# Five stores issued from SyncE's queue instead of ScalarE's

## The chip, the cores and the metric

The kernel runs on the 8 cores of one Trainium2 chip. Each core does the same program on its own data; there is no traffic between cores. The metric is the device time of the slowest core in microseconds.

## The reference

An input x of 4 x 8192 x 1024 (float32) goes through four blocks, each with a layernorm in front and a residual sum behind:

```python
# LN is a layernorm over the last axis
proj = LN(x) @ W_proj.T;  delta, Bs, Cs, residual = split(proj, 4)
delta = softplus(delta @ W_delta.T + b_delta)
y = exp(delta * A) * B * sum_t(xn * Cs) + cumsum_t(delta * B) * sum_t(Cs)
x = x + y + residual * D                       # scan block
x = x + LN(x) @ (W + up @ lora @ down).T + b   # feed forward
q, k, v = LN(x) @ Wq.T + bq, ... Wk ..., ... Wv ...
x = x + softmax(q @ k.T / 32) @ v              # attention over 8192 positions
x = x + LN(x) @ (W + up @ lora @ down).T + b   # feed forward again
```

## The kernel before

Two cores share one of the four sequences. Each core computes keys and values for all 8192 positions (64 tiles of 128 rows, `NT`), and queries and output for its own 4096 (32 tiles, `NQ`). Between the stages, intermediate tiles go to scratch tensors in device memory (names that begin with `sc_`) and are loaded again.

The program is written as lists, one for each engine. `Sched.add` puts an instruction and the semaphore waits ahead of it at the end of an engine's list, and each engine works through its own list in order. `dma(q, out, in, waits, ch)` (L171; every issue is recorded as L177) puts a transfer into the list of "sync" (the SP queue) or of "scalar" (the ACT queue, which ScalarE's own sequencer issues between its computations); `ch` is the semaphore that counts its landing. So the order in which the Python code calls `add` and `dma` is the order of every queue, and a transfer that has to wait stands in front of everything that was added later to the same engine.

Stages, in order of time:

1. *Weights*, loaded through SP and cast by POOL (GpSimd), to about 330 us.
2. *First stage*, 64 tiles (`p1B`, to about 1290 us): three projections on TensorE; softplus of delta on ScalarE (L440, L442); column sums. Each tile stores `sc_delta` (L446) and `sc_res` (L472), both through ACT. The loads of x (`xb`) go through SP, five tiles ahead, and the layernorm of tile i+3 stands behind the store of `sc_res` of tile i on ScalarE's list.
3. *Scan stage*, 64 tiles (`p2A` to `p2C`, to about 3500 us). All of its transfers are on SP.
4. *Query projection* (to about 3735 us), 8 groups of 4 tiles. `prep_group` loads normalized tiles (`xq_in`, SP), transposes them on TensorE (L186) and copies them on ScalarE (L817). Then come 8 x 8 matmuls (L834) with their evictions on ScalarE (L841), and four stores of `sc_qT` (L847, through ACT). Their pieces in memory are 256 bytes long.
5. *Attention*, 4 rounds (`r` = 0 to `KR`-1 = 3), each over a quarter of the keys. A round begins with keys and values of its 16 tiles (L884, L903; loads of `xq_in` again), and then takes the 32 query tiles as steps. A step has three parts. `qS(step)` issues the load of `qT_t` (SP), from round 1 on the load of `zl` (the running sum of the round before, SP), in round 3 also of `x2l` (SP), and then the scores on TensorE (L944), their maxima on VectorE (L954) and the exponentials on ScalarE (L981). `qB(step)` transposes the probabilities (L1013) and copies them on ScalarE (L1021, L1024). `qC(step)` multiplies by the values (L1037) into `PC`, and VectorE writes `zs` (L1046 in round 0, L1051 after it). In rounds 0 to 2, `qC` ends with the store of `sc_z` (L1060, ACT). In round 3 it goes on with a layernorm, the feed forward matmuls (L1086), VectorE's sum (L1093), POOL's sum `s_out` (L1098) and the store of `out` (L1102, ACT).

The order of the parts differs between rounds:

```python
# rounds 0 to 2                         # round 3
qS(step + 2)                            qC(step)
qB(step + 1)                            qS(step + 2)
qC(step)                                qB(step + 1)
```

So in rounds 0 to 2 TensorE does the scores of step s+3 right after the values of step s; in round 3 it does the scores of step s+2 right after L1086 of step s. The buffer `qT_t` is double: its load for a step waits for the scores two steps earlier. `zl` has three buffers and waits for `zs` three steps earlier.

Of the kernel before, what the change touches and what calls it, by code (L numbers as in the profile page):

```python
# [76 lines left out]
def build(phases=3, dbg=False, cut=None):  # L77
# [31 lines left out]
    sc_delta = dS("sc_delta", [NT, 128, 1024])  # L109
    sc_res = dS("sc_res", [NT, 128, 1024])  # L110
# [4 lines left out]
    sc_qT = dS("sc_qT", [NQ, 128, 8, 128], BF16)  # L115
    sc_z = dS("sc_z", [NQ, 128, 1024])
# [140 lines left out]
    try:  # L257
# [119 lines left out]
        if phases >= 1:  # L377
# [35 lines left out]
            def p1B(i):  # L413
# [29 lines left out]
                    delta_f[pp][:, :], e1_f[pp][:, :], AF.Ln, bias=1.0), (SM(mex),),  # L443
                    inc=("s", 1))
                mk[("sp", i)] = mln
                mk[("dst", i)] = dma("scalar", sc_delta[i, :, :], delta_f[p][:, :], ch=f"sdl{p}")  # L446
                mcb = sch.add("scalar", lambda e, pp=p: e.copy(cs_bf[pp][:, :], PB[:, :]),
                              (TM(mcs), GM(mk.get(("m", i - 1), 0)),
                               TM(mk.get(("colsum", i - 1), 0))), inc=("s", 1))
# [10 lines left out]
                for n in range(2):  # L460
                    for k in range(8):
# [7 lines left out]
                    res_f[pp][:, :], PA[:, :]),  # L469
                    (TM(mrs), mk.get(("rst", i - 2))), inc=("v", 1))  # L470
                mk[("resev", i)] = mrev
                mk[("rst", i)] = dma("scalar", sc_res[i, :, :], res_f[p][:, :], (VM(mrev),),  # L472
                                     ch=f"sre{p}")
                mcl = None
                for n in range(2):
# [309 lines left out]
        if phases >= 3:  # L785
# [41 lines left out]
            for g in range(8):  # L827
                pg = g % 2
                mev = prep_group(range(4 * g, 4 * g + 4), pg)
                for c in range(8):  # L830
                    half = c % 2
                    mq = None
                    for k in range(8):
                        mq = sch.add("tensor", lambda e, cc=c, kk=k, hh=half, pp=pg: e.matmul(  # L834
                            PA[:, hh * 512:(hh + 1) * 512],
                            WqT[:, kk * 1024 + cc * 128: kk * 1024 + (cc + 1) * 128],
                            xg3T[pp][:, kk, :], start=(kk == 0), stop=(kk == 7)),
                            ((SM(mev), GM(mwq)) if c == 0 else
                             (SM(mk3.get(("qev", g, c - 2), 0)),)) if k == 0 else (),
                            inc=("t", 1) if k == 7 else None)  # L840
                    mqe = sch.add("scalar", lambda e, cc=c, hh=half, pp=pg: e.activation(  # L841
                        qsp[pp][:, cc, :], PA[:, hh * 512:(hh + 1) * 512],
                        AF.Identity, bias=s_bqT[:, cc:cc + 1], scale=1.0),
                        (TM(mq), mk3.get(("qst", g - 2))), inc=("s", 1))
                    mk3[("qev", g, c)] = mqe
                for t in range(4):
                    mk3[("qst", g)] = dma("scalar", sc_qT[4 * g + t, :, :, :],  # L847
                                          qsp[pg][:, :, t * 128:(t + 1) * 128],
                                          (SM(mk3[("qev", g, 7)]),) if t == 0 else (),
                                          ch=f"sq{pg}")  # L850
# [23 lines left out]
            for r in range(KR):  # L874
# [154 lines left out]
                def qC(step):  # L1029
                    qi = step - r * NQ  # L1030
                    p = step % 2
                    ac = 3 + 3 * (step % 2)
                    mpe = mk3[("pev", step)]
                    mpv = None
                    for j in range(16):
                        for n in range(2):
                            mpv = sch.add("tensor", lambda e, jj=j, nn=n, pp=p: e.matmul(  # L1037
                                PC[:, nn * 512:(nn + 1) * 512], pt_sb[pp][:, jj, :],
                                v_res[:, jj * 1024 + nn * 512: jj * 1024 + nn * 512 + 512],
                                start=(jj == 0), stop=(jj == 15)),  # L1040
                                ((SM(mpe), VM(mk3.get(("zco", step - 1), 0)),
                                  VM(mk3.get(("mo1", step - 1), 0)))
                                 if (j == 0 and n == 0) else ()),
                                inc=("t", 1) if (j == 15 and n == 1) else None)
                    if r == 0:
                        mz = sch.add("vector", lambda e, pp=p: e.tensor_copy(zs[pp][:, :],  # L1046
                                                                             PC[:, :]),
                                     (TM(mpv), mk3.get(("zst", step - 2))), inc=("v", 1))
                    else:
                        mz = sch.add("vector", lambda e, pp=p, z3=step % 3, a_=ac:  # L1050
                                     e.scalar_tensor_tensor(  # L1051
                            zs[pp][:, :], zl[z3][:, :], pstat[:, a_:a_ + 1], PC[:, :],
                            ALU.mult, ALU.add),
                            (TM(mpv), mk3.get(("lz", step)), SM(mk3[("al", step)]),
                             mk3.get(("zst", step - 2)),
                             GM(mk3.get(("moo", step - 2), 0))),
                            inc=("v", 1))
                    mk3[("zco", step)] = mz
                    if r < KR - 1:
                        mk3[("zst", step)] = dma("scalar", sc_z[qi, :, :], zs[p][:, :],  # L1060
                                                 (VM(mz),), ch=f"sz{p}")
                    else:
                        mli = sch.add("vector", lambda e, q_=qi: e.reciprocal(
                            pstat[:, 5:6], l_run[:, q_:q_ + 1]),
                            (mk3[("lr", step)],), inc=("v", 1))
                        mx3 = sch.add("vector", lambda e, pp=p: e.scalar_tensor_tensor(
                            x3b[pp][:, :], zs[pp][:, :], pstat[:, 5:6], x2l[pp][:, :],
                            ALU.mult, ALU.add),
                            (VM(mli), mk3.get(("lx2", step)),
                             GM(mk3.get(("moo", step - 2), 0))), inc=("v", 1))  # L1070
                        mk3[("x3", step)] = mx3
                        if dbg:
                            mk3[("zdbg", step)] = dma("scalar", sc_z[qi, :, :], zs[p][:, :],
                                                      (VM(mx3),), ch=f"sz{p}")
                        mxn4 = ln(x3b[p], xn4b[p], st4[p],
                                  (VM(mx3), TM(mk3.get(("tp4", step - 1), 0))))
                        mtp4 = transposes8(PT1, xn4b[p], (SM(mxn4),))
                        mk3[("tp4", step)] = mtp4
                        mev4 = sch.add("scalar", lambda e, pp=p: e.copy(xn4T[pp],
                                                                        PT1[:, :, :]),  # L1080
                                       (TM(mtp4),), inc=("s", 1))
                        mk3[("ev4", step)] = mev4
                        mf2 = None
                        for n in range(2):
                            for k in range(8):
                                mf2 = sch.add("tensor", lambda e, nn=n, kk=k, pp=p: e.matmul(  # L1086
                                    PC[:, nn * 512:(nn + 1) * 512], xn4T[pp].tensor[:, kk, :],
                                    W_eff[:, kk * 1024 + nn * 512: kk * 1024 + nn * 512 + 512],
                                    start=(kk == 0), stop=(kk == 7)),
                                    (SM(mev4), VM(mk3[("zco", step)])) if (n == 0 and k == 0)  # L1090
                                    else (),
                                    inc=("t", 1) if (n == 1 and k == 7) else None)
                        mo1 = sch.add("vector", lambda e, pp=p: e.tensor_add(  # L1093
                            zs[pp][:, :], PC[:, :], s_bfbc[:, :]),
                            (TM(mf2), GM(mk3.get(("moo", step - 2), 0)),
                             mk3.get(("zdbg", step))), inc=("v", 1))
                        mk3[("mo1", step)] = mo1
                        moo = sch.add("gpsimd", lambda e, pp=p: e.tensor_add(  # L1098
                            s_out[pp][:, :], zs[pp][:, :], x3b[pp][:, :]),
                            (VM(mo1), mk3.get(("ost", step - 1))), inc=("g", 1))  # L1100
                        mk3[("moo", step)] = moo
                        mk3[("ost", step)] = dma("scalar", out_d[qi * 128:(qi + 1) * 128, :],  # L1102
                                                 s_out[p][:, :], (GM(moo),), ch=f"so{p}")

                qS(r * NQ)
# [138 lines left out]
```

How the kernel before makes its waits and increments, by code:

```python
        def f(eng):  # L1144
            for item in sch.prog[name]:
                if item[0] == "w":
                    eng.wait_ge(sems[item[1]], item[2])
                else:
                    _, fn, inc = item
                    ins = fn(eng)
                    if inc is not None:
                        ins.then_inc(sems[inc[0]], inc[1])
```

## Time and profile before

| | us |
|---|---|
| median of 2 runs | 7386.89 |
| the two runs | 7283.85, 7489.93 |
| the profiled execution | 7288.19 |
| its span (slowest core, core 1) | 7286.6 |
| spans of the 8 cores | 7252.1 to 7286.6 |
| mean granted TensorE clock, each core | 0.784 |

The span is the time from the first to the last instruction of the slowest core; the profiled execution's time has 1.6 us around it. Busy shares over the whole span are TensorE 60%, ScalarE 34%, VectorE 22%, POOL 18%. They are averages over stages with different limits, so the stages have to be read apart. The granted clock is the share of full speed (2.4 GHz) that TensorE was given; 0.5 is 1.2 GHz. In the rows, SPq and ACTq are the issues of transfers by SP and by ScalarE. Us to landing is the time from the issue to the arrival of the data.

### The profile page before, as it was taken

What the parts mean: (1) busy time and instruction counts of PE and PEld (TensorE: products, weight loads), DVE (VectorE), ACT (ScalarE), POOL (GpSimd) and SP (SyncE); (2) the same over time, 40 slices, a digit from 0 to 9 for tenths busy, and PEclk for the clock granted to TensorE, in tenths of its full rate; (3) what the DMA queues carried; (4) which work ended last, traced back from release to release, by engine and by line L of the source; (5) the groups of instructions that cost most, each with busy time, mean ns of one, the idle gap of its engine ahead of it and who ended that gap; (6) DMA issues with size and microseconds to landing.
All of it is one profiled execution on the core that took longest, in us unless ns stands there. A gap on an engine that the chain in (4) does not pass through costs nothing.

```text
span 7286.6 us, 65385 instructions; the slowest of 8 cores (7252.1 to 7286.6 us)
## 1 busy us (share of the span) xinstructions
PE 4391.3 (60%) x20288; PEld 1954.9 (27%) x20288; DVE 1639.0 (22%) x2744; ACT 2501.2 (34%) x4418; POOL 1323.1 (18%) x611
## 2 busy tenths in 40 slices
PE   3788887122222222222578997999899865555555
PEld 1333333000000000000234443444344322222222
DVE  0322222122222222222002221332233122222221
ACT  0555553133333333333323342333233223222222
POOL 2222222443344344443100000000000000000000
PEclk8899998555555555555789999999999977777777
DMA  4222221311211111111221111222122101111110
GB/s 131 93 98 96 96 99 68 117 65 65 75 69 65 65 61 51 61 51 52 69 52 36 55 53 38 79 87 73 45 87 88 59 35 41 41 41 41 41 48 25
DMA packets 183211, 475.82 MB, mean 65 GB/s; under 512 B 51149, under 2 KB 51278, under 8 KB 182868
## 3 DMA queue, kind: packets, MB, share of 16 engines
q1 hardware_dynamic: 112564, 328.75, 14.2%
q10 hardware_dynamic: 70304, 142.89, 5.0%
q8 instruction: 168, 2.75, 0.2%
q14 instruction: 175, 1.43, 0.1%
HBM read 295.12 MB, written 176.42 MB: 65 GB/s over the span
## 4 chain that ended last, share of the span: by engine, by line
PE 46%; ACT 17%; POOL 11%; DVE 10%; DMA 8%; issue 5%; SPq 2%; ACTq 1%; DVEq 0%; POOLq 0%
PE PC L1037 13%; PE PA L944 6%; PE PB L944 6%; DMA p2B<-sc_delta 5%; PE PA L884 3%; PE PB L903 3%; PE PA L420 3%; PE PC L1086 3%; PE PT L186 2%; POOL p2g L650 2%; POOL p2D L644 2%; POOL p2D L673 2%; POOL g_bf L451 2%; ACT L208 2%; DVE st L191 2%
## 5 line engine op out<-in xcount | busy, mean ns | idle before, releaser
L1037 PE MATMUL PC<-v_res,pt_sb 128*128 128x512 bf16 x4096 | 994.8, 405 | 285.3 <-ACT pt_sb L1024 280.1
L1098 POOL TENSOR_TENSOR s_out<-zs,x3b 128x1024 f32<-128x1024 f32 x32 | 75.0, 2343 | 3695.9 <-DVE zs L1093 3695.9
L1037 PEld LDWEIGHTS PC<-v_res,pt_sb 128*128 128x128 bf16 x4096 | 415.3, 103 | 813.9 <-issue 412.3
L186 PE MATMUL PT<-s_id,xn2b 128*128 128x128 bf16 x512 | 64.8, 307 | 755.4 <-ACT xn2b L212 755.4
L944 PE MATMUL PA<-kT_res,qT_t 128*128 128x512 bf16 x2048 | 470.7, 384 | 28.5 <-ACT P_bf L981 22.6
L944 PE MATMUL PB<-kT_res,qT_t 128*128 128x512 bf16 x2048 | 462.9, 379 | 0.0
L712 PE MATMUL PB<-W_eff,xn2T 128*128 128x512 bf16 x1024 | 361.5, 531 | 85.5 <-ACT xn2T L700 84.0
L644 POOL TENSOR_TENSOR p2D<-p2B,s_A1bc 128x1024 f32<-128x1024 f32 x64 | 149.6, 2338 | 1014.4 <-DMA p2B<-sc_delta 1013.8
L655 PE MATMUL PA<-p2g,s_tri 128*128 128x512 bf16 x64 | 32.4, 609 | 455.1 <-POOL p2g L650 455.1
L648 ACT ACT_TABLE_LOAD x61 | 78.3, 1283 | 643.8 <-POOL p2D L644 643.8
L451 POOL TENSOR_TENSOR g_bf<-delta_f,s_B1bc 128x1024 bf16<-128x1024 f32 x64 | 150.0, 2344 | 794.4 <-ACT delta_f L442 794.4
L944 PEld LDWEIGHTS PA<-kT_res,qT_t 128*128 128x128 bf16 x2048 | 201.5, 99 | 277.6 <-issue 43.0
L903 PE MATMUL PB<-WvT,xg3T 128*128 128x512 bf16 x1024 | 231.3, 379 | 71.3 <-DVE v_res L913 71.3
L420 PE MATMUL PA<-W_dd,xnT 128*128 128x512 bf16 x1024 | 268.8, 422 | 3.5 <-DVE xnT L409 3.5
L884 PE MATMUL PA<-xg3T,WkT 128*128 128x512 bf16 x1024 | 253.0, 413 | 23.5 <-ACT xg3T L817 23.5
L186 PEld LDWEIGHTS PT<-s_id,xn2b 128*128 128x128 bf16 x512 | 49.6, 138 | 810.5 <-issue 810.5
L944 PEld LDWEIGHTS PB<-kT_res,qT_t 128*128 128x128 bf16 x2048 | 200.4, 98 | 241.7
L655 PE MATMUL PC<-p2g,s_tri 128*128 128x512 bf16 x64 | 32.4, 609 | 385.4 <-POOL p2g L650 385.4
L913 DVE TENSOR_TENSOR v_res<-PB,s_bvbc 128x1024 bf16<-128x1024 f32 x64 | 78.4, 1225 | 811.9 <-PE PB L903 811.9
L954 DVE TENSOR_REDUCE cmax<-PB 128x1 f32<-128x512 f32 x256 | 177.1, 692 | 263.7 <-PE PB L944 263.7
L1051 DVE SCALAR_TENSOR_TENSOR zs<-zl,pstat,PC 128x1024 f32<-128x1024 f32 x96 | 122.9, 1280 | 487.9 <-PE PC L1037 487.9
L434 PE MATMUL PB<-WcT,xnT 128*128 128x512 bf16 x1024 | 231.5, 379 | 0.0
(164 smaller groups left out, 6929.9 us busy)
## 6 DMA issues: line engine op xcount, KB each, us to landing
sc_z<-zs ACTq DMA_DIRECT2D x96, 512.0 KB, 4.7
zl<-sc_z SPq DMA_DIRECT2D x96, 512.0 KB, 5.0
xb<-x SPq DMA_DIRECT2D x64, 512.0 KB, 3.5
sc_delta<-delta_f ACTq DMA_DIRECT2D x64, 512.0 KB, 2.6
sc_res<-res_f ACTq DMA_DIRECT2D x64, 512.0 KB, 2.6
p2A<-x SPq DMA_DIRECT2D x64, 512.0 KB, 4.9
p2B<-sc_delta SPq DMA_DIRECT2D x64, 512.0 KB, 5.6
p2C<-sc_res SPq DMA_DIRECT2D x64, 512.0 KB, 6.5
```

Source lines behind the costliest of these rows:

```text
L186: e.transpose(o, i_, s_id[:, :]),
L420: mdp = sch.add("tensor", lambda e, nn=n, kk=k, qq=q3: e.matmul(PA[:, nn * 512:(nn + 1) * 512], xnT[qq][:, kk, :], W_dd[:, kk * 1024 + nn ...
L434: mcs = sch.add("tensor", lambda e, nn=n, kk=k, qq=q3: e.matmul(PB[:, nn * 512:(nn + 1) * 512], xnT[qq][:, kk, :], WcT[:, kk * 1024 + nn * ...
L451: mg0 = sch.add("gpsimd", lambda e, pp=p: e.tensor_mul(g0_bf[pp][:, :], delta_f[pp][:, :], s_B1bc[:, :]), (SM(mln), TM(mk.get(("colsum", i ...
L644: mei = sch.add("gpsimd", lambda e, pp=p: e.tensor_mul(D_[pp][:, :], B_[pp][:, :], s_A1bc[:, :]), (VD(mk2[("ldl", i)]), GM(mr2) if i == 0 ...
L712: mf1 = sch.add("tensor", lambda e, nn=n, kk=k, pp=p: e.matmul(PB[:, nn * 512:(nn + 1) * 512], xn2T[pp][:, kk, :], W_eff[:, kk * 1024 + nn ...
L884: mq = sch.add("tensor", lambda e, cc=c, kk=k, hh=half, pp=pg: e.matmul(PA[:, hh * 512:(hh + 1) * 512], WkT[:, kk * 1024 + cc * 128: kk * ...
L903: mv = sch.add("tensor", lambda e, nn=n, kk=k, tt=t, pp=pg: e.matmul(PB[:, nn * 512:(nn + 1) * 512], xg3T[pp][:, kk, tt * 128:(tt + 1) * 128],
L944: e.matmul(o[:, of:of + 512], qT_t[pp][:, cc, :], kT_res[:, cc, nn * 512:(nn + 1) * 512], start=(cc == 0), stop=(cc == 7)),
L954: mrx = sch.add("vector", lambda e, nn=n, o=ps_, of=off: e.reduce_max(cmax[:, nn:nn + 1], o[:, of:of + 512], AX), (TM(msmm),), inc=("v", 1))
L1037: mpv = sch.add("tensor", lambda e, jj=j, nn=n, pp=p: e.matmul(PC[:, nn * 512:(nn + 1) * 512], pt_sb[pp][:, jj, :], v_res[:, jj * 1024 + n ...
L1086: mf2 = sch.add("tensor", lambda e, nn=n, kk=k, pp=p: e.matmul(PC[:, nn * 512:(nn + 1) * 512], xn4T[pp].tensor[:, kk, :], W_eff[:, kk * 10 ...
```

## The change

Five stores go into SP's list instead of ScalarE's, at the same places of the program: `sc_delta` and `sc_res` of each tile of the first stage, the four `sc_qT` of each group of the query projection, `sc_z` of each step of rounds 0 to 2, and `out` of each step of round 3. The store of `sc_delta`, which had stood behind its producer on ScalarE itself, gets an explicit wait for it; the other stores keep the waits they had. The two small stores `sc_hi` and `sc_lo` stay on ACT.

```diff
-                mk[("dst", i)] = dma("scalar", sc_delta[i, :, :], delta_f[p][:, :], ch=f"sdl{p}")
+                mk[("dst", i)] = dma("sync", sc_delta[i, :, :], delta_f[p][:, :],
+                                     (SM(mln),), ch=f"sdl{p}")
...
-                mk[("rst", i)] = dma("scalar", sc_res[i, :, :], res_f[p][:, :], (VM(mrev),),
+                mk[("rst", i)] = dma("sync", sc_res[i, :, :], res_f[p][:, :], (VM(mrev),),
                                      ch=f"sre{p}")
...
                 for t in range(4):
-                    mk3[("qst", g)] = dma("scalar", sc_qT[4 * g + t, :, :, :],
+                    mk3[("qst", g)] = dma("sync", sc_qT[4 * g + t, :, :, :],
                                           qsp[pg][:, :, t * 128:(t + 1) * 128],
                                           (SM(mk3[("qev", g, 7)]),) if t == 0 else (),
                                           ch=f"sq{pg}")
...
                     if r < KR - 1:
-                        mk3[("zst", step)] = dma("scalar", sc_z[qi, :, :], zs[p][:, :],
+                        mk3[("zst", step)] = dma("sync", sc_z[qi, :, :], zs[p][:, :],
                                                  (VM(mz),), ch=f"sz{p}")
...
-                        mk3[("ost", step)] = dma("scalar", out_d[qi * 128:(qi + 1) * 128, :],
+                        mk3[("ost", step)] = dma("sync", out_d[qi * 128:(qi + 1) * 128, :],
                                                  s_out[p][:, :], (GM(moo),), ch=f"so{p}")
```

## Rows read from the trace of the kernel before

**Rows 1.** The page, granted TensorE clock in 40 slices of the span, in tenths

```profile
PEclk8899998555555555555789999999999977777777
```

**Rows 2.** Stretches (rounds 0, 1, 3): length, PE, PEld, DVE, ACT, POOL, clock, DMA

```profile
3900.00:4370.00 470.00, 461.12 (x2495) 223.34 (x2494) 136.51 (x223) 181.16 (x413) 0.00 (x0) 1.00 0.15 51
...
4580.00:5050.00 470.00, 461.70 (x2515) 224.75 (x2516) 152.90 (x335) 183.38 (x406) 0.00 (x0) 0.99 0.26 88
...
6600.00:7286.00 686.00, 374.07 (x1578) 161.97 (x1576) 142.46 (x268) 190.33 (x357) 37.48 (x16) 0.73 0.11 38
```

**Rows 3.** Timeline of a step of round 1: start, duration (us), engine, line, operation

```profile
4729.47 3.62 PE L944 MATMUL PA<-kT_res,qT_t 128*128 128x512 bf16 x16
4729.88 1.28 DVE L1051 SCALAR_TENSOR_TENSOR zs<-zl,pstat,PC 128x1024 f32<-128x1024 f32 x1 [1.31 <-PE PC L1037]
...
4731.29 0.32 SPq L177 DMA_DIRECT2D zl<-sc_z  x1
...
4731.71 0.38 SPq L177 DMA_DIRECT2D qT_t<-sc_qT  x1
...
4744.18 3.62 PE L944 MATMUL PA<-kT_res,qT_t 128*128 128x512 bf16 x16
```

**Rows 4.** Chain of waits in the same step: start, duration, engine, tile, line

```profile
4722.73 6.91 PE PC L1037 x32
4729.63 3.45 PE PA L944 x16
```

**Rows 5.** Timeline, a step of round 0

```profile
4004.67 1.23 DVE L1046 COPY zs<-PC 128x1024 f32<-128x1024 f32 x1 [2.58 <-PE PC L1037]
```

**Rows 6.** Tile qT_t, issue to landing: round 0, round 1, round 3

```profile
DMA to landing us min/median/max: 2.5/2.6/3.1
...
DMA to landing us min/median/max: 4.6/5.0/6.1
...
DMA to landing us min/median/max: 3.6/4.1/4.9
```

**Rows 7.** Timeline, a step of round 3

```profile
6508.02 9.95 PE L1037 MATMUL PC<-v_res,pt_sb 128*128 128x512 bf16 x32 [8.85 <-ACT pt_sb L1024]
...
6529.93 5.78 PE L1086 MATMUL PC<-W_eff,pt_sb 128*128 128x512 bf16 x16 [1.36 <-ACT pt_sb L1079]
...
6535.55 3.62 PE L944 MATMUL PA<-kT_res,qT_t 128*128 128x512 bf16 x16
...
6537.25 2.35 POOL L1098 TENSOR_TENSOR s_out<-zs,x3b 128x1024 f32<-128x1024 f32 x1 [42.00 <-DVE zs L1093]
...
6539.68 0.34 ACTq L177 DMA_DIRECT2D out<-s_out  x1
```

**Rows 8.** Stretches of the query projection, columns as in rows 2

```profile
3601.40:3606.80 5.40, 0.05 (x2) 0.04 (x2) 0.00 (x0) 1.02 (x2) 0.00 (x0) 0.90 1.00 243
3606.80:3610.20 3.40, 2.02 (x16) 1.51 (x16) 0.00 (x0) 3.03 (x3) 0.00 (x0) 0.50 0.60 154
```

**Rows 9.** Timeline between two groups of the query projection

```profile
3601.41 4.13 ACTq L177 DMA_DIRECT2D sc_qT<-qsp  x4
3605.64 4.47 ACT L817 COPY xg3T<-PT 128x1024 bf16<-128x1024 bf16 x4 [4.30 <-issue]
3606.80 2.16 PE L186 MATMUL PT<-s_id,xq_in 128*128 128x128 bf16 x16 [5.35 <-ACT xg3T L817]
```

**Rows 10.** Chain of waits from round 0 into the projection of round 1

```profile
4389.38 0.91 PE PT L186 x16
...
4390.35 3.69 DMA xq_in<-sc_xn
```

**Rows 11.** Timeline, a tile of the first stage

```profile
805.76 16.91 SPq L177 DMA_DIRECT2D xb<-x  x2
...
814.61 0.33 ACTq L177 DMA_DIRECT2D sc_res<-res_f  x1
816.16 1.06 ACT L193 ACTIVATE s_sqscr<-xb 128x1024 bf16<-128x1024 f32 x1 [3.45 <-POOL m_bf L455]
```

## Prediction, on record before the change was run

> **What bounds the kernel now.** I read the views in this order: the clock line of the page, the busy times by stage, one step of the attention in order of time, the chain of waits of the same step, and then the issue-to-landing times of the query load.
>
> The clock line [rows 1] shows a kernel of several stages: high in the first fifth, low in the middle (the scan stage, which this change does not touch), full in three blocks of the attention, and about 0.73 in the last one. The stage table [rows 2] says what limits each. In rounds 0, 1 and 2 of the attention TensorE is busy for 461 of 470 us at the full clock: it is the bound, and whatever makes it wait is added to the end. In round 3 it is busy for 374 of 686 us, at 0.73: there TensorE, VectorE and ScalarE hand one tile to each other in a chain, so a delay of a link is added too.
>
> One step of round 1 [rows 3] is where the change decides. The queue of SP issues `zl` when VectorE has written `zs`, and 0.42 us later `qT_t`. That `qT_t` is not for the matmuls that run at this moment. They began at 4729.47, before it was issued; it is for the scores one step (14.71 us) later. The chain [rows 4] shows it: the last value matmul at 4722.73 takes 6.91 us and the scores follow at 4729.63 with no wait between. All of the load's landing time is hidden by a step of work.
>
> **The change, part by part.** Nothing is computed differently. Five stores leave ScalarE's queue for SP's, and SP works through its list in order: an issue that waits holds up every later one.
>
> *Rounds 0 to 2, `sc_z`.* Order on TensorE: scores(s+3) right behind values(s). Order on SP from now on: the store of step s, which waits for `zs`(s), and behind it the loads of `qT_t`(s+3) and `zl`(s+3). In the kernel before, `qT_t`(s+3) stood behind a wait for step s-1 at most. Now it stands behind one for step s, whose result comes after the very matmul that the scores follow. So scores(s+3) wait: from the end of the values at 4729.63 to the start of `zs` 0.25 us, `zs` itself 1.28, its signal to the issue 0.13, the store's place in the queue 0.42 (the spacing of two issues), then the landing L, then 0.13 to start TensorE (an estimate, the same as from `zs` to the issue): 2.2 us + L [rows 3, 4]. In round 0 the eviction is 1.23 us [rows 5], which gives 2.16 + L.
>
> L is read from the landing times of this same load [rows 6]: 2.6 us alone (round 0), 4.1 behind one other 512 KB transfer on its queue (round 3), 5.0 with a 512 KB load ahead of it and a 512 KB store beside it (rounds 1 and 2). The new queue has one 512 KB store ahead and, from round 1 on, `zl` behind: that is round 3's pattern, so 4.1. In round 0 nothing follows it, and I take the middle of 2.6 and 4.1, 3.4. The bounds are 2.6 and 5.0.
>
> [...]
>
> Stalls: 2.16 + 3.4 = 5.6 us in round 0, 2.2 + 4.1 = 6.3 in rounds 1 and 2. In each round the first store stands behind the load for its third step, so 29 loads (steps 3 to 31) are late: 29 x 5.6 = 162, 58 x 6.3 = 365.
>
> *The clock.* A wait of this length costs more than itself. In the query projection TensorE sat idle for 5.35 us [rows 9]; the granted clock of that stretch was 0.90, so it fell from full to half towards its end, and was 0.50 after it [rows 8]. 0.50 is 1.2 GHz, 1.00 is 2.4. What a fall costs is seen in round 3 [rows 7]: 32 value matmuls after an idle stretch took 9.95 us where 32 at the full clock took 6.91 [rows 4], 3.0 more; 16 of L1086 took 5.78 against half of 6.91, 2.3 more. I take 2.3 for each stall, because some waits may end before the clock is down; bounds are nothing and 3.0. That is 87 x 2.3 = 200.
>
> *Round 3, `out`.* SP's order there is the store of `out`(s), which waits for POOL's `s_out`, then `qT_t`(s+2), needed as soon as the matmuls of L1086 end at 6535.7 [rows 7]. POOL's sum starts at 6537.25 and takes 2.35, the issue follows at 6539.68, the load 0.42 later, L = 4.1, 0.13 to start: 6544.35, or 8.65 us later than before. 30 steps are so (2 to 31): 30 x 8.65 = 260, and 30 x 2.3 = 69 for the clock. The wait of the value matmuls for ScalarE in the same step does not hide it, since that one starts from the scores' end.
>
> *Between rounds.* The first input load of the key and value projection now stands behind the last `sc_z` store. Before, TensorE went from the values into two transposes at once, and waited 3.69 us for the third load [rows 10]. Now: 0.25 + 1.23 + 0.13 + 0.42 + 4.1 + 0.13 = 6.3 us ahead of the first transpose, none of it covered. 3 x 6 = 18.
>
> *Query projection, `sc_qT`.* Here ScalarE gains. Four issues in a row take 4.13 us of it, and the copy for which TensorE waits starts only after them [rows 9]. But the two next loads of `xq_in` now stand behind these issues: issued from 3605.6 on instead of ahead of them. The stores, 4.13 us of issues at a DMA share of 1.00 [rows 8], are still draining. A 256 KB load alone lands in 2.6 us [rows 6]; with one to two us of queue before it (my choice, within the 4.13 of the issues), it lands near 3610, and two transposes and copies (1.1 us each) later the projection starts near 3613.5 instead of 3610.3, the end of the four copies [rows 9]. 7 groups x 3.3 = 23 us lost, where a load that found the queue empty would lose 1.
>
> *First stage, `sc_delta` and `sc_res`.* Nothing either way. ScalarE's next work, at 816.16, was released by POOL's `m_bf`, 1.2 us after the `sc_res` issue of 814.61 was over [rows 11], and `m_bf` stands behind POOL's `g_bf`, which waits for the softplus and for no issue: the 0.33 us issues were off the chain. The load of `xb` goes from 805.8 to about 815 in its tile, and is used two tiles later, each 16.6 us (the two issues of [rows 11] span 16.91, less one issue); if that cover were gone, the landing time of a load would count in each tile, some 3 to 5 us by [rows 6].
>
> **Sum.** 162 + 365 + 200 + 260 + 69 + 18 + 23 = 1097. The profiled execution took 7288.19 us, so 8385. The median of the two runs shown, 7386.89, is 98.7 above that execution, of which nothing is in the sum.
>
> **Rivals.**
> - *The queue order does not hold the load (other side).* If `qT_t` lands before the values end, no stall exists, and what remains is ScalarE's time: 8 x 4.13 = 33 us in the query projection give 7255, no change by the bound below; all of the other 256 issues at 0.33 us on the chain as well would give 84 more and 7171, 1.6% under this execution and 2.9% under the median shown. It decides at the point where the landing is earlier than 4729.63 on the clock of [rows 3]. For it speaks that SP idles most of the step; against it that an issue in order behind a wait for `zs` cannot precede `zs`, which ends at 4731.16. Chance 0.04 for 7255, 0.01 for 7171 or less.
> - *The same by a rule.* The Trainium skill, page "DMA: Bandwidth & Descriptors", section "Issuing engines are not separate DMA queues", holds that SP and ACT feed the same 16 engines, so that the choice saves only issue time. By that rule the result is the 7255 of the rival above. The trace agrees on bandwidth and says nothing for the order of the waits, which is what moves here.
> - *Stalls without the clock.* The waits come, but the clock stays up: 1097 - 269 = 828, so 8116. For it: in rounds 0 to 2 TensorE is busy for two thirds of the longer step too, where round 3 has it busy for 55% at 0.73 [rows 2]. Against it: the 5.35 us wait of [rows 9]. Chance 0.15.
> - *Slow landings.* L = 5.0 and 3.0 for the clock: 29 x 10.2 + 58 x 10.2 + 30 x 12.55 = 1264, with 41 for the rest 1305, so 8593. For it: the landing in rounds 1 and 2. Against it: the store is no longer beside the load on another queue. Chance 0.15.
> - *Forecast* as summed, 0.65.
>
> The lowest sum, L = 2.6 and no clock, is 87 x 4.8 + 30 x 7.1 + 10 = 641, so 7930. The range 8060 to 8610 takes in the forecast, the slow landings and most of the case without the clock. About 2% is what a measurement here can tell from no change. Chances: faster 0.01, same 0.04, slower 0.95.
>
> **What would show it.** In the profile after: TensorE idle before L944 `PA`, released by the DMA `qT_t<-sc_qT`, 117 times in the attention, 5 to 9 us each; steps of some 22.5 to 23.5 us instead of 14.7 in rounds 0 to 2, and some 11 us longer in round 3; the clock of rounds 0 to 2 well under 1.00; SP waiting for VectorE's `zs` and for POOL's `s_out`; the first and the scan stage unchanged within 1%. A period of 14.7 in round 1 would prove the order argument wrong; stalls of the right size with matmuls at the full clock the clock term; a query projection that got shorter the last term.

## The result and the profile after

The changed kernel took 8427.0 us (median of 11 runs, 8335.4 to 8464.1), the kernel before 7371.1 us (median of 10 runs). The ratio is 1.151, 95% interval 1.145 to 1.158: 15% slower. The two medians are 1.06 ms apart. In some executions of any of these kernels the cores of one die show a lower granted clock and take some per cent longer; every ratio in this document leaves those out, the medians do not. The profiled execution took 8374.73 us. Its slowest core was core 7 (mean clock 0.755, core 1 has 0.764). What follows compares core 1 with core 1, spans 8318.7 and 7286.6 us, a difference of 1032 us.

The page of the changed kernel's slowest core, the clock line and the two queues (packets, MB, share of the DMA engines' time):

```profile
PEclk8999985555555555578888888888888876766776
...
q1 hardware_dynamic: 182708, 471.37, 16.7%
...
q10 hardware_dynamic: 160, 0.26, 0.0%
```

ACT's queue (q10) is empty but for two small stores. The three blocks of full clock of [rows 1] are gone: rounds 0 to 2 of the attention run at 8 tenths. Here are the rounds of [rows 2] again, rounds 0, 1 and 3 as a whole on core 1 (length, PE, PEld, DVE, ACT, POOL, clock, DMA share, GB/s):

```profile
3961.00:4631.00 670.00, 507.48 (x2400) 227.20 (x2400) 126.60 (x206) 168.70 (x379) 0.00 (x0) 0.88 0.11 36
...
4841.00:5525.00 684.00, 511.79 (x2403) 228.03 (x2400) 147.41 (x321) 169.59 (x380) 0.00 (x0) 0.88 0.17 58
6629.00:8295.00 1666.00, 813.04 (x3192) 337.85 (x3192) 286.70 (x548) 389.72 (x732) 72.45 (x31) 0.70 0.10 34
```

In rounds 0 and 1 TensorE is busy for 75 to 76% of the time, where it was busy for 98%, and at 0.88 instead of 1.00. What it waits for is told by the view of who waited for whom (engine, tile and line, releaser, us in total, times, longest):

```profile
PE PA L945 <- DMA qT_t<-sc_qT: 743.6, 117, 8.8
```

That wait did not exist before. 117 is 3 x 29 + 30. One such step of round 1 in order of time, to be held against [rows 3]:

```profile
5209.99 1.28 DVE L1052 SCALAR_TENSOR_TENSOR zs<-zl,pstat,PC 128x1024 f32<-128x1024 f32 x1 [1.30 <-PE PC L1038]
5211.35 0.32 SPq L177 DMA_DIRECT2D sc_z<-zs  x1
5211.76 0.38 SPq L177 DMA_DIRECT2D qT_t<-sc_qT  x1
5212.23 0.74 SPq L177 DMA_DIRECT2D zl<-sc_z  x1
...
5215.43 6.43 PE L945 MATMUL PA<-kT_res,qT_t 128*128 128x512 bf16 x16 [5.68 <-DMA qT_t<-sc_qT]
```

The load of `qT_t` leaves at the same point as in [rows 3], right after `zs`. But it now serves the scores that should run at that moment, not those a step later. TensorE stands for 5.68 us, and the 16 matmuls behind the wait take 6.43 us instead of 3.62 (as a median of the late steps 6.0). In round 3 the load stands behind the store of `out`:

```profile
7739.74 2.34 POOL L1099 TENSOR_TENSOR s_out<-zs,x3b 128x1024 f32<-128x1024 f32 x1 [52.35 <-DVE zs L1094]
7742.15 0.34 SPq L177 DMA_DIRECT2D out<-s_out  x1
7742.60 0.36 SPq L177 DMA_DIRECT2D qT_t<-sc_qT  x1
...
7746.99 5.30 PE L945 MATMUL PA<-kT_res,qT_t 128*128 128x512 bf16 x16 [8.79 <-DMA qT_t<-sc_qT]
```

This wait of 8.79 us is the longest of the 30 in round 3; their median is 7.94, and the 16 matmuls behind them take 5.7 us as a median.

Where the time came from, by stage, on core 1 (us; `delta_f` is VectorE's writing of it in L427, and a round is taken from its first `zs` to its last):

| stage | before | after | difference |
|---|---|---|---|
| first stage, first to last `delta_f` | 1029.0 | 1030.6 | +2 |
| last result of the scan to first `v_res` (query projection) | 258.7 | 276.2 | +18 |
| round 0 | 443.8 | 670.7 | +227 |
| round 1 | 444.0 | 683.7 | +240 |
| round 2 | 444.0 | 684.0 | +240 |
| round 3 | 1364.8 | 1665.9 | +301 |
| last `zs` of a round to next `v_res`, 3 times | 79.7 | 96.7 | +17 |

These are 1045 us. The scan stage was 11 us shorter in this execution; it has no instruction of the change in it.

### The profile page after: what moved, and what is told of

Its sections match the earlier page's. It is cut to its first block, busy times and chain, and to the rows that moved or that the text cites. A ratio compares the mean times of both kernels' runs of the same rounds, so it can differ in the third digit from the quotient of the medians.

```text
span 8373.2 us, 65331 instructions; the slowest of 8 cores (8303.1 to 8373.2 us)
## 1 busy us (share of the span) xinstructions
PE 4717.7 (56%) x20288; PEld 2023.4 (24%) x20288; DVE 1639.3 (20%) x2744; ACT 2501.2 (30%) x4418; POOL 1323.0 (16%) x611
## 4 chain that ended last, share of the span: by engine, by line
PE 44%; ACT 14%; DMA 12%; DVE 10%; POOL 10%; issue 5%; SPq 2%; DVEq 0%; ACTq 0%; POOLq 0%
PE PC L1038 12%; PE PA L945 9%; PE PB L945 5%; DMA qT_t<-sc_qT 5%; DMA p2B<-sc_delta 4%; PE PA L885 3%; PE PB L904 3%; PE PA L420 3%; PE PC L1087 2%; SPq L177 2%; PE PT L186 2%; POOL p2g L651 2%; POOL p2D L645 2%; POOL p2D L674 2%; POOL g_bf L452 2%
## 5 line engine op out<-in xcount | busy, mean ns | idle before, releaser
L945 PE MATMUL PA<-kT_res,qT_t 128*128 128x512 bf16 x2048 | 734.3, 537 | 775.0 <-DMA qT_t<-sc_qT 746.8
L945 PEld LDWEIGHTS PA<-kT_res,qT_t 128*128 128x128 bf16 x2048 | 256.0, 129 | 1252.3 <-issue 1203.6
L955 DVE TENSOR_REDUCE cmax<-PA 128x1 f32<-128x512 f32 x256 | 177.1, 692 | 1216.4 <-PE PA L945 1215.2
L968 ACT ACTIVATE pstat<-pstat 128x1 f32<-128x1 f32 x96 | 19.5, 203 | 1094.3 <-DVE pstat L966 1093.9
```

The source lines that it names most:

```text
L945: e.matmul(o[:, of:of + 512], qT_t[pp][:, cc, :], kT_res[:, cc, nn * 512:(nn + 1) * 512], start=(cc == 0), stop=(cc == 7)),
L955: mrx = sch.add("vector", lambda e, nn=n, o=ps_, of=off: e.reduce_max(cmax[:, nn:nn + 1], o[:, of:of + 512], AX), (TM(msmm),), inc=("v", 1))
```

## The experiments

Two theories could explain a loss of this kind. **Order:** the load of `qT_t` stands in SP's list behind a store that waits, so it is issued too late; how much the store moves is beside the point. **Sharing:** with 143 MB more on one queue, the loads meet the stores and arrive late. Both would show TensorE waiting for `qT_t`. The first four kernels move one kind of store each (the two of the first stage together), the fifth moves none, and the sixth moves all but in another order. A seventh is about the clock alone.

### One kind of store at a time

From the kernel before, `sc_z` alone:

```diff
-                        mk3[("zst", step)] = dma("scalar", sc_z[qi, :, :], zs[p][:, :],
+                        mk3[("zst", step)] = dma("sync", sc_z[qi, :, :], zs[p][:, :],
```

> The kernel before with the store of sc_z alone on SP. Theory A (order: the load of qT_t is held behind the store that waits for zs): the loss of rounds 0 to 2 and of the three round changes appears whole, about 227 + 240 + 240 + 17 = 724 us as the profiles of before and after show it, so about 8010 us against 7288; round 3 keeps its 44.35 us step. Theory B (sharing: what costs is that all traffic is on one queue): sc_z is only 50 MB of the 143 MB that moved, so about a third of the loss, some 350 us, 7640 us.

Measured: ratio to before 1.106 (1.092 to 1.121), fastest run 8022.5 us. On core 1 rounds 0 to 2 took 676, 687 and 684 us, the three changes of round 98.1 instead of 79.7, and round 3 took 1364.8 as before. The loss is the whole one of these rounds, not a third of it.

`out` alone:

```diff
-                        mk3[("ost", step)] = dma("scalar", out_d[qi * 128:(qi + 1) * 128, :],
+                        mk3[("ost", step)] = dma("sync", out_d[qi * 128:(qi + 1) * 128, :],
```

> The kernel before with the store of out alone on SP. Theory A: the loss of round 3 whole, 301 us, so about 7590 us, steps of 54.6 us in round 3 and of 14.71 us in rounds 0 to 2. Theory B: out is 17 MB of the 143 MB that moved, some 120 us, 7410 us.

Measured: ratio 1.041 (1.035 to 1.048), fastest run 7580.1 us. Round 3 took 1665.9 us on core 0, exactly as in the changed kernel, with a median step of 54.56; rounds 0 to 2 kept 14.71.

`sc_qT` alone:

```diff
-                    mk3[("qst", g)] = dma("scalar", sc_qT[4 * g + t, :, :, :],
+                    mk3[("qst", g)] = dma("sync", sc_qT[4 * g + t, :, :, :],
```

> The kernel before with the four sc_qT stores of each group alone on SP. Theory A: 18 us lost in the query projection (the loads of xq_in wait behind the issues and the traffic of the stores), 7306 us, not to be told from no change by the time alone; in the profile the groups take some 28.3 us where before has 26.0. The rival says that ScalarE, rid of four issues of 4.13 us in each group, gains 33 us, 7255 us, with groups of 22 us.

Measured: ratio 1.0014 (0.9987 to 1.0042), fastest run 7293.1 us, no difference by the time. In the profile it is there: from the last result of the scan to the first `v_res` 276.0 us against 258.7, and 28.4 us from group to group against 25.9. Why ScalarE's gain does not show is seen in the timeline of the changed kernel, SP and TensorE of its core 7 between two groups (the others have the same pattern):

```profile
3579.94 1.06 PE L186 MATMUL PT<-s_id,xq_in 128*128 128x128 bf16 x16
...
3580.96 3.22 SPq L177 DMA_DIRECT2D sc_qT<-qsp  x4
...
3584.28 6.69 SPq L177 DMA_DIRECT2D xq_in<-sc_xn  x4
3588.71 1.86 PE L186 MATMUL PT<-s_id,xq_in 128*128 128x128 bf16 x16 [7.71 <-DMA xq_in<-sc_xn]
...
3592.12 16.02 PE L835 MATMUL PA<-xg3T,WqT 128*128 128x512 bf16 x64 [1.55 <-ACT xg3T L818]
```

The second pair of transposes waited 5.35 us for ScalarE in [rows 9]; now it waits 7.71 us for the load, which stands behind the four stores.

`sc_delta` and `sc_res` alone:

```diff
-                mk[("dst", i)] = dma("scalar", sc_delta[i, :, :], delta_f[p][:, :], ch=f"sdl{p}")
+                mk[("dst", i)] = dma("sync", sc_delta[i, :, :], delta_f[p][:, :],
+                                     (SM(mln),), ch=f"sdl{p}")
-                mk[("rst", i)] = dma("scalar", sc_res[i, :, :], res_f[p][:, :], (VM(mrev),),
+                mk[("rst", i)] = dma("sync", sc_res[i, :, :], res_f[p][:, :], (VM(mrev),),
```

> The kernel before with the stores of sc_delta and sc_res alone on SP: 84 MB of the 143 MB that moved. Both the order argument and the first stage's chain say no change: 7288 us within 0.3%, first stage within 3 us of its 1029. Theory B (sharing of one queue) would put the largest part of the loss here, some 600 us; if ScalarE's issues were on the chain it would be 42 us faster.

Measured: ratio 1.003 (0.999 to 1.007), fastest run 7278.6 us; the first stage took 1028.9 us. My expectation had the bytes wrong: 128 stores of 512 KB are 67 MB, not 84. So nearly half of the moved bytes cost nothing that can be measured. The four losses add up to the whole: 0.106 + 0.041 + 0.001 + 0.003 = 0.151, and the change measured 0.151. With intervals of up to 0.015 on each side, agreement to the last digit is chance; that they add up is not.

### The wait without the store

The kernel before, every store where it was. Only the load of `qT_t` gets one more wait, for the `zs` behind which the changed kernel puts it:

```diff
-                              (TM(mk3.get(("smm", step - 2), 0)), mk3[("qst", qi // 4)]),
+                              (TM(mk3.get(("smm", step - 2), 0)), mk3[("qst", qi // 4)],
+                               VM(mk3.get(("zco", step - 3), 0))
+                               if (r < KR - 1 and qi >= 3) else None),
```

> The kernel before, all stores on ACT as they were, but the load of qT_t in rounds 0 to 2 waits for zs of the step whose values the scores follow (from the fourth step of a round on). Nothing shares SP's queue that did not before. Theory A: the wait is the cause, and the store ahead in the queue adds only its 0.42 us issue and a part of the landing. TensorE waits 1.74 us + landing of 2.6 to 5.0, about 5 us, and the clock falls as in after (2.5 us a step): 87 x 7.5 = 650 us more, about 7940 us. Theory B (sharing of the queue with the stores): no change, 7288 us.

Measured: ratio 1.101 (1.091 to 1.111), fastest run 7996.4 us. A step of round 1:

```profile
5190.00 1.28 DVE L1053 SCALAR_TENSOR_TENSOR zs<-zl,pstat,PC 128x1024 f32<-128x1024 f32 x1 [1.03 <-PE PC L1039]
5191.36 0.36 ACTq L177 DMA_DIRECT2D sc_z<-zs  x1
5191.36 0.32 SPq L177 DMA_DIRECT2D qT_t<-sc_qT  x1
5191.78 0.38 SPq L177 DMA_DIRECT2D zl<-sc_z  x1
5195.40 5.96 PE L946 MATMUL PA<-kT_res,qT_t 128*128 128x512 bf16 x16 [5.65 <-DMA qT_t<-sc_qT]
```

This settles it for rounds 0 to 2. The store is on ACT's queue, at the same moment, and TensorE waits 5.65 us where the changed kernel has 5.68. The load leaves 0.4 us earlier, with no store in front, and lands in 3.7 us beside the store. In the changed kernel it lands in 3.4 us behind the store. Counted from the issue of the store, that is the same: 3.7 and 3.8 us. The steps took 22.8 to 22.9 us. The three rounds lost 698 us on core 1, my estimate was 650: I had the wait at about 5 us, and it is 5.7.

### The same queue, another order

This is the changed kernel with all five kinds of store on SP. Those of `sc_z`, `out` and `sc_qT` are held back and put into the list behind the loads that follow; `sc_delta` and `sc_res` stay where the change had put them:

```diff
-                        mk3[("zst", step)] = dma("sync", sc_z[qi, :, :], zs[p][:, :],
-                                                 (VM(mz),), ch=f"sz{p}")
+                        def zstore(step=step, qi=qi, p=p, mz=mz):
+                            mk3[("zst", step)] = dma("sync", sc_z[qi, :, :], zs[p][:, :],
+                                                     (VM(mz),), ch=f"sz{p}")
+                        pend.append(zstore)
...
                         if qi + 2 < NQ:
                             qS(step + 2)
+                        flush()     # issues what pend holds
```

The stores of `out` and `sc_qT` are held back in the same way.

> The changed kernel with all five stores on SP, but each one put into SP's list behind the loads of the next step: sc_z behind the loads of the step after, out behind the loads for step s+2, the four sc_qT behind the loads of the next group; the last sc_z of a round behind the first input loads of the next. Same traffic on the same queue. Theory A (order of waits): all stalls go; steps of 14.71 and 44.35 us, and the query projection gains what ScalarE's four issues cost, 8 x 4 us: 7288 - 33 = 7255 us, ratio to before about 0.995. Theory B (sharing of one queue): the loads still meet the stores, the loss stays by a half or more, over 7800 us.

Measured: ratio to before 0.9965 (0.9938 to 0.9992), median 7283.8 against 7300.3 us, fastest run 7248.8. Steps took 14.71 and 44.35 us. A step of round 1 on core 1:

```profile
4799.65 3.62 PE L955 MATMUL PA<-kT_res,qT_t 128*128 128x512 bf16 x16
4800.06 1.28 DVE L1062 SCALAR_TENSOR_TENSOR zs<-zl,pstat,PC 128x1024 f32<-128x1024 f32 x1 [1.30 <-PE PC L1048]
4801.48 0.32 SPq L177 DMA_DIRECT2D zl<-sc_z  x1
...
4801.85 0.42 SPq L177 DMA_DIRECT2D sc_z<-zs  x1
4802.37 0.38 SPq L177 DMA_DIRECT2D qT_t<-sc_qT  x1
...
4814.36 3.62 PE L955 MATMUL PA<-kT_res,qT_t 128*128 128x512 bf16 x16
```

A `qT_t` still leaves right behind a store, but again it is the one for the scores a step later. It also lands later than in the kernel before, in 5.8 us as a median of round 1 instead of 5.0, and that costs nothing, because it still lands some 6 us before it is needed. No wait for `qT_t` is left in any round. So the loss of the change was order, all of it. What is left over is a small gain of 0.35%, too small to be told by the time alone. In the profile two places are shorter. One is round 3, 1358.7 us against 1364.8; why was not looked into. The larger one is the query projection: 239.1 us from the scan to the first `v_res` against 258.7 before. ScalarE's four issues are gone, and the loads are ahead of the stores. Two groups of it (from the timeline of core 1):

```profile
3608.34 1.06 PE L186 MATMUL PT<-s_id,xq_in 128*128 128x128 bf16 x16
3609.02 5.62 SPq L177 DMA_DIRECT2D xq_in<-sc_xn  x4
...
3612.58 1.67 PE L186 MATMUL PT<-s_id,xq_in 128*128 128x128 bf16 x16 [3.19 <-DMA xq_in<-sc_xn]
...
3614.74 3.82 SPq L177 DMA_DIRECT2D sc_qT<-qsp  x4
3615.68 15.98 PE L841 MATMUL PA<-xg3T,WqT 128*128 128x512 bf16 x64 [1.44 <-ACT xg3T L823]
```

A group takes 23.2 us against 25.9 before. I had expected 4 us less, the issues in full. They do not come in full because the loads for the second pair of transposes become the next limit: 3.19 us of wait in the rows.

### The clock term alone

This is the changed kernel with useless matmuls placed in the waits; the scores overwrite their result:

```diff
+                    nfill = 0
+                    if r < KR - 1 and qi >= 3:
+                        nfill = 22
+                    if r == KR - 1 and qi >= 2:
+                        nfill = 36
+                    for f in range(nfill):
+                        sch.add("tensor", lambda e, cc=f % 8: e.matmul(
+                            PA[:, 0:512], kT_res[:, cc, 0:128], kT_res[:, cc, 0:512],
+                            start=True, stop=True),
...
```

> The changed kernel, stalls as they are, but while TensorE would wait for qT_t it does matmuls whose result is overwritten: 22 in each late step of rounds 0 to 2 (4.75 us at the full clock, in waits of 5.6) and 36 in round 3 (7.8 in 8.8). Theory of the clock term: the clock no longer falls in these waits, so a step is the old step plus the bare wait: 14.71 + 5.6 = 20.3 us in rounds 0 to 2 (from 22.8 to 23.3) and 44.35 + 8.8 = 53.1 in round 3 (from 54.6), together 275 us less than the changed kernel, about 8100 us. Rival: the scores are slow behind the wait for another reason (the operands have just arrived, loads and stores run beside them): no gain, 8375 us or more.

Measured: ratio to before 1.111 (1.101 to 1.121), where the change has 1.151; the profiled core 1 span was 8008.9 us. A step of round 1, and round 1 as a stretch:

```profile
5100.10 4.91 PE L945 MATMUL PA<-kT_res 128*128 128x512 bf16 x22
...
5102.28 0.38 SPq L177 DMA_DIRECT2D qT_t<-sc_qT  x1
...
5105.65 3.61 PE L956 MATMUL PA<-kT_res,qT_t 128*128 128x512 bf16 x16 [0.63 <-DMA qT_t<-sc_qT]
```

```profile
4771.00:5385.00 614.00, 583.46 (x3036) 274.38 (x3034) 147.44 (x322) 169.14 (x379) 0.00 (x0) 1.00 0.19 64
```

The data arrives as late as before, but the scores behind it run at the full clock, 3.61 us instead of 6.43. The rival (slow because of the transfers beside them) is out. The rounds took 604.5, 614.2 and 614.8 us: 66, 70 and 69 less than in the changed kernel, 2.3 to 2.4 us in each of 29 steps. What is left over the 444 of before, 161 to 171 us, is 5.5 to 5.9 us for a step, the bare wait. In round 3 the gain was 102 us, not the 43 I expected. There more than the scores became faster: over the round the clock was 0.80 instead of 0.70, the value matmuls of a step took 8.97 us instead of 9.83 and L1087's (L1098 in this kernel) 5.34 instead of 5.72. Both are also faster than in the kernel before, where [rows 7] has 9.95 and 5.78. So in round 3 this run gives back more than the change had cost, and it does not isolate the clock term there.

## Why the prediction was right

8385 us was forecast, 8427 measured as a median, 8375 in the profiled execution. Term by term, with the measured side on core 1:

| term | forecast | measured |
|---|---|---|
| wait for `qT_t`, round 0 | 29 x 5.6 = 162 | 29 x 5.56 = 161 |
| the same, rounds 1 and 2 | 58 x 6.3 = 365 | 170 + 171 = 341 |
| the same, round 3 | 30 x 8.65 = 260 | 242 |
| clock, rounds 0 to 2 | 87 x 2.3 = 200 | 66 + 70 + 69 = 205 |
| clock, round 3 | 30 x 2.3 = 69 | 301 - 242 = 59 |
| between rounds | 18 | 17 |
| query projection | 23 | 18 |
| first stage | 0 | +2 |

- **The order argument held.** It rests on reading two lists beside each other: what TensorE does next, and which load for it stands behind which wait. The count came out as forecast, 117 late loads, and so did the step: the wait alone makes it, and the order alone undoes it.
- **The landing was mis-sized.** I took 4.1 us for rounds 1 to 3 from a load that stood behind another load [rows 6]. Behind a store it is 3.3 to 3.5 us as a median in every round, with or without `zl` behind it:

```profile
DMA to landing us min/median/max: 3.2/3.3/3.7
...
DMA to landing us min/median/max: 3.2/3.4/4.3
```

  (The tile `qT_t` of the changed kernel, round 0 and round 1, core 1.) The waits came out 43 us smaller than forecast. The Trainium skill's page "DMA: Bandwidth & Descriptors", section "Anatomy of one DMA", fits a DMA that GpSimd issues as about 2.0 us plus its bytes at 436 GB/s. Taken over to these transfers, which SP issues, that is an estimate of 3.8 us for store and load together, or 3.4 from the load's own issue, and these rows agree.
- **The rule on issuing engines.** By the section "Issuing engines are not separate DMA queues" of the Trainium skill's page "DMA: Bandwidth & Descriptors", only issue time should change. For the bandwidth the runs agree (the same five stores on SP, three of them moved behind the loads, cost nothing). As a forecast for this change the rule fails by 15%, because that section says nothing of the waits in the list.
- **The clock term held**, 264 us against 269. In rounds 0 to 2 the run with matmuls in the waits shows size and cause. In round 3 the 59 us are what is left of the loss after the waits. The rows bear them out: the 16 matmuls behind a wait take 5.7 us as a median instead of 3.6, about 2.1 us more in each of 30 steps, while the value matmuls and L1087's took as long as before (9.9 and 5.8 us). The evidence beforehand was a single wait of 5.35 us and the granted clock around it [rows 8, 9], so the size came out better than that evidence could promise.
- **The rivals.** "The queue order does not hold the load" is refuted by the 117 waits. "Stalls without the clock" would have been 8116 us. The clock did fall, so that is refuted. The run with matmuls in the waits makes that case on purpose, and its profiled execution took 8011 us: the waits are shorter than I had them, and round 3 gained more than its clock term. "Slow landings" did not occur, the longest median of a round was 3.5 us.
- **Nothing in the first stage**, as read from [rows 11]; its own run confirms it.
- **In the query projection** the sign was right and the size 5 us off. The loads left earlier than I had put them: four issues that took 4.13 us of ScalarE [rows 9] took 3.22 us of SP (the row at 3580.96 above).

The median of the change lies 52 us above its profiled execution, as the median of the runs of before lay above its own. The sum was made against the profiled execution, so its 8385 has to be held against 8375. That these agree to 10 us is in part luck. On core 1 the loss was 1032 us, 65 less than the sum of 1097: 52 of them are the differences in the table, and 11 the shorter scan stage. The slowest core of the profile, core 7, was 55 us longer than core 1 at a slightly lower clock, and that made up for the landing that I had too long.

## What to carry to other kernels

Before moving a transfer to another queue, write down the two lists that it joins and leaves, and for each transfer behind it ask when its data is needed. A store that waits for the last result of a step must not stand ahead of a load for the next one: here that cost 15%, and the same stores on the same queue, a few list entries later, cost nothing. Where the waiting engine is TensorE, price the wait with the slow matmuls behind it: here 2.3 to 2.4 us on top of each 5.5 to 5.9.

## What the runs showed of the hardware

- A 256 KB load landed in 3.4 us behind a 512 KB store on its own queue, issued 0.4 us after it, and in 3.7 us when both were issued at once on two queues. From the store's issue that is 3.8 and 3.7 us: sharing the queue made no difference to the arrival.
- The clock cost about the same behind a wait of 5.6 us and one of 8 us, 2.3 and 2.0 us (the second is what is left of round 3's loss after its waits). Keeping TensorE busy in the wait with useless matmuls made rounds 0 to 2 205 us shorter; the granted clock was 1.00 in them.
- In round 3 the matmuls put into the wait for `qT_t` also made two later groups of the step faster, the value matmuls by 0.9 us and L1087's by 0.4, although TensorE sat idle for 9.1 us ahead of the first and 9.6 us ahead of the second. Why was not tested.
